# The first feed-forward layer in two batches, and attention prepared sequence by sequence

## The chip, the cores and the metric

The kernel runs on one core of a Trainium2 chip. TensorE (PE) multiplies matrices and transposes, VectorE (DVE), ScalarE (ACT) and GpSimd (POOL) work on tiles of 128 partitions, SyncE (SP) issues most transfers, and every engine takes its own instructions in order. Semaphores tie the engines together. The metric is the time of one execution on the device in microseconds, the median of several.

## The reference

The input x holds 8 sequences of 256 tokens with 128 features. Three layers follow one another, each on the layer-normalised x and added to x:

```
x = x + 0.5 * ffn(layernorm(x))
x = x + attention(layernorm(x))
x = x + 0.5 * ffn(layernorm(x))
```

`ffn` sends each token to one of 8 experts (the arg-max of a softmax over 8 gate logits), computes relu(x W1 + b1) W2 + b2 of that expert (hidden size 512) and scales it by the gate's probability. `attention` applies an RMS norm, makes q, k and v for 16 heads of 8 features, takes a causal softmax within each sequence, projects, and adds the normalised input.

## The kernel before

Tokens stand in 16 tiles of 128 (`row`, `x`, two tiles to a sequence).

**First feed-forward layer.** The 16 tiles are normalised, gated and routed in three chunks (`route_pick`, `route_prob`, `route_slot`). POOL writes each tile's rows to memory, sorted by expert (`dispatch`, L462), ScalarE pads every expert's region, and VectorE makes a table of at most 23 sorted tiles of one expert each (`tile_table`, NS = 16 + 8 - 1). TensorE fills the time until all have landed with products of zeros (`idle_work`, L1207: 35, then 9 after the landing).

**Expert tiles.** SyncE loads sorted tiles into a ring of 12 (L362). For tile t ScalarE normalises (L615), TensorE transposes (`turn`, L1271), ScalarE copies back (L621), TensorE multiplies by W1 in four pieces (`hidden`, L1279), ScalarE and VectorE apply the relu (L627, L923), TensorE multiplies by W2 (`output`, L1290), VectorE adds the bias (L939), scales and adds x (`scale`, L947, done one iteration later, after the bias of tile t + 1), and POOL scatters the tile's rows to `x_d` (L470). VectorE copies the weights three tiles ahead (L931). TensorE's order is turn(t + 2), hidden(t + 1), output(t). Transposed tiles go to banks 0 and 1, outputs to banks 6 and 7, in turns.

**Between.** When all rows are scattered, SyncE loads x back (L408). Five units of 2, 2, 4, 4, 4 tiles are normalised (statistics on VectorE L801, power on POOL L454), transposed (L1339), multiplied into q, k (`quad_qk`, L1346) and v (`quad_v`, L1354), split into three bf16 parts (L680, L687, L1014, L1028), stored to `sp_d` by SyncE (`split_stores`, L383 and L384, four issues a sequence) and loaded back as stacks (`stack_load`, L397, four issues a half).

**Attention.** Step b of 8 has two halves of six units. TensorE makes the transposed scores of sequence b (`scores_k`, L1408 and L1414) and, for the maxima, the scores of sequence b + 1 (`scores_q`, L1381 to L1393); VectorE takes maxima (L1038, L1042), POOL splits them (`max_split`), TensorE turns them (`turn_max`, L1445), ScalarE copies them and SyncE loads them as extra rows of the stack (`max_rows`, L402): the first scores_k of a half waits for that transfer. ScalarE takes exponentials (L723), POOL masks (L541), TensorE multiplies by v (L1432, L1436). Steps 1 to 4 are a hardware loop. POOL also adds up the residual (L500 to L504). SyncE's order in step b is: `max_rows(b, 1)`, `stack_load(b + 2, 0)`, `max_rows(b + 1, 0)`, stores of a later sequence where one is due, `stack_load(b + 2, 1)`.

**Second feed-forward layer.** Its routing runs beside the last steps, and 23 expert tiles follow.

## Time and profile before

| what | us |
|---|---|
| median of three runs | 322.5 (321.55 to 323.66) |
| span of the profiled execution | 319.3 |
| first expert tiles | 41.6 to 84.9 |
| attention steps 0 to 7 | 127.5 to about 240 |
| second expert tiles | 264.5 to 308 |
| busy in the span: TensorE, VectorE, POOL, ScalarE | 276.5, 214.5, 178.8, 159.7 |

The profile gives the times of every instruction in one execution; a row of a timeline is one instruction or a run of like ones, and a bracket at its end says how long its engine had been idle and what ended the wait. TensorE's rows end later than its next one begins, since products overlap; what a product costs TensorE is read from start to start. PEclk is the clock granted to TensorE, 1.00 for 2.4 GHz and 0.50 for 1.2 GHz.

### The profile page before, as it was taken

Reading aid. Unit: us, or ns where it says so; the run is one execution under the profiler, and the core shown is the slowest. Engines: PE = TensorE matmul, PEld = TensorE weight load, DVE = VectorE, ACT = ScalarE, POOL = GpSimd, SP = SyncE. Lnnn points to the kernel's source line nnn. Section 1 sums busy time; section 2 is a strip of 40 time slices with the busy share of each in tenths; the row PEclk is TensorE's granted clock in tenths of the full one; section 3 lists DMA queues with packets and bytes.
Section 4 is the critical chain, followed back from the end, with each engine's and each line's share of the span. In section 5 each row is a group of like instructions: output and inputs, shape, how many; then the busy total and the mean of one; then the engine's idle time right before and its main releaser. Section 6 shows DMA issues by size and latency. Waiting matters only on the chain.

```text
span 319.3 us, 7990 instructions
## 1 busy us (share of the span) xinstructions
PE 276.5 (87%) x2396; PEld 224.1 (70%) x2396; DVE 214.5 (67%) x691; ACT 159.7 (50%) x389; POOL 178.8 (56%) x319
## 2 busy tenths in 40 slices
PE   8573999999995776999999999998977699999960
PEld 8463999999994363656666566665646588999960
DVE  3877048788608759987666777776787555888850
ACT  2430076666204834586666667768541107666620
POOL 5577815554525201587777787788657730554551
PEclk9855999999999998799999999999976579999996
DMA  6973141220040731662524522110001143222100
GB/s 180 403 293 119 53 95 54 65 63 31 24 126 8 199 121 53 197 180 88 156 79 134 152 72 74 57 53 6 3 19 42 42 121 86 51 67 71 34 10 0
DMA packets 34387, 29.37 MB, mean 92 GB/s; under 512 B 4108, under 2 KB 28817, under 8 KB 34352
## 3 DMA queue, kind: packets, MB, share of 16 engines
q1 hardware_dynamic: 29696, 23.52, 24.6%
q0 software_dynamic: 2496, 4.27, 4.1%
q10 hardware_dynamic: 2160, 1.14, 1.4%
q8 instruction: 18, 0.29, 0.4%
q14 instruction: 17, 0.14, 0.2%
HBM read 17.08 MB, written 12.55 MB: 93 GB/s over the span
## 4 chain that ended last, share of the span: by engine, by line
PE 58%; POOL 11%; DVE 10%; issue 7%; DMA 5%; ACT 4%; POOLq 1%; ACTq 0%; SPq 0%; DVEq 0%
PE bank L1279 13%; PE bank L1290 12%; PE bank L1207 5%; PE bank L1436 3%; PE bank L1408 3%; PE bank L1384 3%; POOL pT L541 2%; POOL row L454 2%; PE bank L1381 2%; PE bank L1414 2%; PE bank L1271 2%; POOL disp_d L462 2%; PE bank L1240 2%; PE bank L1466 2%; PE bank L1389 1%
## 5 line engine op out<-in xcount | busy, mean ns | idle before, releaser
L723 ACT ACTIVATE pT<-bank 128x512 f32<-128x512 f32 x96 | 56.4, 599 | 36.2 <-PE bank L1414 25.2
L1207 PE MATMUL bank<-zero 128*128 128x128 f32 x298 | 43.2, 314 | 9.4 <-DVE rowi L916 4.7
L1279 PE MATMUL bank<-xsT,ew 128*128 128x128 f32 x368 | 48.8, 276 | 0.2
L1290 PE MATMUL bank<-experts,hT 128*128 x368 | 48.9, 276 | 0.0
L1207 PEld LDWEIGHTS bank<-zero 128*128 128x128 f32 x298 | 41.6, 227 | 10.1 <-DVE rowi L916 4.7
L1038 DVE TENSOR_REDUCE mh<-bank 128x2 f32<-128x512 f32 x64 | 42.1, 682 | 8.5 <-PE bank L1384 8.2
L541 POOL TENSOR_SCALAR_AFFINE_SELECT pT<-pT 128x512 f32<-128x512 f32 x62 | 39.8, 643 | 10.2 <-ACT pT L723 9.9
L1279 PEld LDWEIGHTS bank<-xsT,ew 128*128 128x128 f32 x368 | 44.7, 192 | 0.7 <-ACT xsT L621 0.3
L1290 PEld LDWEIGHTS bank<-experts,hT 128*128 128x128 f32 x368 | 44.8, 192 | 0.5 <-issue 0.3
L627 ACT ACTIVATE hT<-bank,ew 128x128 f32<-128x128 f32 x92 | 28.8, 364 | 28.9 <-PE bank L1279 28.9
L923 DVE TENSOR_SCALAR hT<-bank,ew 128x128 f32<-128x128 f32 x92 | 28.0, 346 | 20.2 <-PE bank L1279 18.9
L470 POOL DMA_INDIRECT out<-ys_sb,xs_sb x23 | 22.5, 980 | 30.8 <-DVE ys_sb L947 30.2
L462 POOL DMA_INDIRECT disp_d<-row,slot x32 | 31.6, 988 | 13.6 <-issue 9.4
L470 POOL DMA_INDIRECT x_d<-ys_sb,xs_sb x23 | 22.7, 986 | 25.8 <-DVE ys_sb L947 25.1
L615 ACT ACTIVATE xq<-xs_sb 128x128 f32<-128x128 f32 x46 | 22.6, 492 | 26.5 <-DMA xs_sb<-disp_d 26.5
L1042 DVE TENSOR_REDUCE mh<-bank 128x4 f32<-128x512 f32 x32 | 22.1, 690 | 18.8 <-PE bank L1393 18.6
L1408 PE MATMUL bank<-qz,ks 99*128 99x512 bf16 x64 | 25.2, 396 | 0.4 <-DMA qz<-mT 0.3
L1384 PE MATMUL bank<-ks,qz 96*128 96x256 bf16 x128 | 25.4, 281 | 0.0
L931 DVE TENSOR_SCALAR ew<-experts 128x644 f32 x46 | 22.2, 491 | 2.2 <-issue 1.6
L585 ACT ACTIVATE xn<-row 128x128 f32<-128x128 f32 x23 | 10.6, 490 | 24.2 <-DVE row L813 24.2
L1436 PE MATMUL bank<-pT,va 128*32 128x256 f32 x256 | 20.9, 398 | 1.8 <-DVE pT L1164 1.4
L939 DVE TENSOR_TENSOR yb<-bank,ew 128x128 f32<-128x128 f32 x46 | 13.4, 291 | 12.7 <-PE bank L1290 10.0
(133 smaller groups left out, 479.4 us busy)
## 6 DMA issues: line engine op xcount, KB each, us to landing
sp_d<-spl SPq DMA_DIRECT2D x32, 192.0 KB, 2.6
experts<-in_experts SPq DMA_DIRECT2D x8, 578.0 KB
qz<-sp_d SPq DMA_DIRECT2D x32, 96.0 KB
ks<-sp_d SPq DMA_DIRECT2D x32, 96.0 KB
xs_sb<-disp_d SPq DMA_DIRECT2D x46, 66.0 KB, 1.8
row<-in_x SPq DMA_DIRECT2D x4, 256.0 KB, 5.5
row<-x_d SPq DMA_DIRECT2D x4, 256.0 KB, 5.0
disp_d<-pad ACTq DMA_DIRECT2D x12, 66.0 KB, 2.3
```

What stands on the lines that cost most here:

```text
L462: pool.indirect_dma_start(disp_d[f][:, :], bass.IndirectOffsetOnAxis(ap=slot[:, t:t + 1], axis=0), row[:, t, :], None).then_inc(d_tok[f], 16)
L470: pool.indirect_dma_start(target[:, :], bass.IndirectOffsetOnAxis(ap=xs_sb[:, t % RING, ID:ID + 1].bitcast(U32), axis=0), ys_sb[:, t % OUT ...
L541: pool.affine_select(out=p_, in_=p_, pattern=[[0, 4], [1, P]], compare_op=ALU.is_ge, fill=0.0, base=0, channel_multiplier=-1).then_inc(a_p ...
L627: mm = act.activation(hT[:, par, c, :], bank[2 + 2 * par][:, c * P:(c + 1) * P], ACT.Relu, bias=ew[:, k, HID + c:HID + c + 1])
L723: act.activation(pT[:, u, :], bank[2 + u % 2][:, :], ACT.Exp, scale=SCALE).then_inc(a_e, 1)
L1038: dve.tensor_reduce(mh[:, half, 1, :, 2 * pp + w], bank[u % 2][:, :].rearrange("p (h n) -> p h n", h=2), AX.X, ALU.max).then_inc(a_mx, 1)
L1207: pe.matmul(bank[b][:, 0:P], zero[:, :], zero[:, :], start=True, stop=True)
L1279: mm = pe.matmul(bank[2 + 2 * (k % 2) + c // 2][:, (c % 2) * P:(c % 2 + 1) * P], ew[:, k % WRING, c * P:(c + 1) * P], xsT[:, k % 2, :], st ...
L1290: mm = pe.matmul(bank[6 + k % 2][:, 0:D], hT[:, k % 2, c, :], w2.rearrange("p a c -> p (a c)"), start=(c == 0), stop=(c == HC - 1))
L1384: mm = pe.matmul(ov[:, j, :], qz[k][0:SROWS, half, j, pair - 4 * half, P:T], ks[k][0:SROWS, pair, :], start=False, stop=True, **MM_BANK)
L1408: mm = pe.matmul(ov, ks[k][0:KROWS, pair, 0:P], qz[k][0:KROWS, half, :, pair - 4 * half, :], start=True, stop=True, **MM_BANK)
L1436: mm = pe.matmul(o[32 * h:32 * h + 32, pp * T:(pp + 1) * T], va[:, k, 0, 8 * j + pair, :], pT[:, 3 * pp + h // 2, j * T:(j + 1) * T], star ...
```

## The change

The 16 tiles of the first feed-forward layer go in two batches of 8, each with its own routing tables, pads and region in memory, and each with up to 15 expert tiles: 30 in one run instead of 23. Batch 1's dispatches, tables and pads are put among the first tiles of batch 0. The transposed tile has one bank (7) and the output one (6). Attention is prepared per sequence, not per unit: statistics on VectorE, power and the normalisation itself on POOL (`seq_normalise`), then transposes, q, k, v and the splits. Sequences 0 to 2 are prepared in tiles 19 to 28 of the run; their x is loaded back once the first 15 tiles are scattered. Sequences 3 to 7 are prepared within attention steps 0 to 4 (sequence b + 3 in step b), in banks 4 and 5, which attention uses too. The repeated copies of the splits in SBUF are dropped; a store of six parts and three of two replace four of three. The loop over steps is unrolled. In the diff, code for the routing tables, semaphore names and the late layer's renumbering is left out.

```diff
+BATCH = [(0, 8), (8, 16), (0, 16)]
+NS = [t1 - t0 + NE - 1 for t0, t1 in BATCH]
+G0 = [sum(NS[:f]) for f in range(len(BATCH) + 1)]
+HEAD = 3
+HEAD_AT = [20, 22, 24]
+HEAD_PE = [(21, 22, 23), (23, 24, 25), (25, 26, 27)]
...
# SyncE
+            def split_stores(b):
+                k = b % SPL
+                sp.wait_ge(q_s2, b + 1)
+                sp.wait_ge(q_spl, b + 1)
+                dst = sp_d[b * 2 * t_rows:(b + 1) * 2 * t_rows, :].rearrange("(m r) n -> r m n", r=P)
+                sp.dma_start(dst[:, 0:6, :], spl[:, k, :, :]).then_inc(q_std[b], 16)
+                for c, src in ((3, slice(0, 4, 3)), (4, slice(2, 6, 3)), (5, slice(0, 6, 5))):
+                    sp.dma_start(dst[:, 2 * c:2 * c + 2, :], spl[:, k, src, :]).then_inc(q_std[b], 16)
...
+            pad_rows(0, range(0, 4))
+            tile_loads(0, NS[0])
+            pad_rows(1, range(0, NE))
+            tile_loads(G0[1], G0[1] + RING)
+            all_scattered(NS[0])
+            reload(range(HEAD))
+            tile_loads(G0[1] + RING, G0[2])
             sp.wait_ge(static_s, 6)
-            split_stores(0, 1)
-            stack_load(0, 0, 0)
-            stack_load(0, 0, 1)
-            stack_load(1, 1, 0)
-            max_rows(0, 0, 0)
-            stack_load(1, 1, 1)
+            split_stores(0)
+            stack_load(0, 0)
+            stack_load(0, 1)
+            split_stores(1)
+            stack_load(1, 0)
+            stack_load(1, 1)
             split_stores(2)
-            stores = {(0, 0): (3,), (0, 1): (4,), (1, 1): (5,), (2, 1): (6,), (3, 1): (7,)}
+            all_scattered(G0[2])
+            reload(range(HEAD, B))
+            max_rows(0, 0)
             for b in range(B):
...
+                max_rows(b, 1)
+                if b + 2 < B:
+                    stack_load(b + 2, 0)
+                if b + 1 < B:
+                    max_rows(b + 1, 0)
+                if b + HEAD < B:
+                    split_stores(b + HEAD)
+                if b + 2 < B:
+                    stack_load(b + 2, 1)
...
# POOL
+            def seq_normalise(b):
+                ln_scale(1, b)
+                pool.wait_ge(ln_rs[1], b + 1)
+                for t in (2 * b, 2 * b + 1):
+                    i1 = pool.tensor_scalar(xn[:, t, :], x[:, t, :], mv[:, t, 0:1], rs[:, t:t + 1],
+                                            ALU.subtract, ALU.mult)
+                i1.then_inc(ln_xn[1], 1)
...
+            dispatch(0, 0, range(0, 4))
+            dispatch(0, 1, range(4, 8))
             stack_fill(1)
+            dispatch(1, 0, range(8, 11))
+            for g in range(G0[1]):
+                scatter_out(x_d, g)
+                if g < 5:
+                    dispatch(1, 0, range(11 + g, 12 + g))
+            for g in range(G0[1], G0[2]):
+                scatter_out(x_d, g)
...
+                if g in HEAD_AT:
+                    seq_normalise(HEAD_AT.index(g))
...
# POOL, attention step
-                if not isinstance(b, int):
-                    pool.tensor_tensor(turn[:, n:n + 1], zero[:, 0:1], zero[:, 0:1], ALU.add)
...
+                    if b + 4 < B and (half, n) == (1, 3):
+                        seq_normalise(b + 4)
             max_split(0, 0)
+            seq_normalise(HEAD)
...
# ScalarE, expert tiles (after tile g) and attention step
+            def head_work(g):
+                for b in range(HEAD):
+                    if g == HEAD_PE[b][1]:
+                        seq_split1(b)
+                    if g == HEAD_PE[b][1] + 1:
+                        seq_split2(b)
+                for b in range(HEAD):
+                    if g == HEAD_PE[b][0]:
+                        seq_copy(b)
...
+                    if b + HEAD < B:
+                        if (half, u) == (0, 5):
+                            seq_copy(b + HEAD)
+                        if (half, u) == (1, 1):
+                            seq_split1(b + HEAD)
+                        if (half, u) == (1, 4):
+                            seq_split2(b + HEAD)
...
# VectorE, expert tiles (after tile g) and attention
+            def early_work(g):
+                if g == 0:
+                    pad_table(1)
+                if 1 <= g <= 4:
+                    tile_table(1, g - 1)
+                for b in range(HEAD):
+                    if g == HEAD_AT[b] - 1:
+                        ln_stats(1, b)
+                    if g == HEAD_PE[b][1]:
+                        seq_rest(b)
+                    if g == HEAD_PE[b][2]:
+                        seq_vbias(b)
+                    if g == HEAD_PE[b][1] + 2:
+                        seq_split3(b)
...
+                    if b + HEAD < B:
+                        if (half, u) == (1, 2):
+                            seq_rest(b + HEAD)
+                        if (half, u) == (1, 5):
+                            seq_split3(b + HEAD)
+                    if 0 < b and b + HEAD - 1 < B and (half, u) == (0, 1):
+                        seq_vbias(b + HEAD - 1)
+                    if b + HEAD + 1 < B and (half, u) == (1, 3):
+                        ln_stats(1, b + HEAD + 1)
...
             for u in range(6):
                 max_unit(0, 1, u)
+                if u == 2:
+                    ln_stats(1, HEAD)
...
# TensorE
             gate_turn(0, 2)
+            logits(0, 2)
             gate_turn(0, 3)
-            logits(0, 2)
-            ranks(0, 1)
             logits(0, 3)
-            ranks(0, 2)
-            counts(0)
-            pe.wait_ge(r_row, 1)
-            idle_work(5, 35)
+            ranks(1, 0)
+            counts(1)
+            pe.wait_ge(r_sm[0], 2)
+            idle_work(6, 35)
             all_dispatched(0)
...
+            def seq_turn(b):
+                pe.wait_ge(ln_xn[1], b + 1)
+                need(pe, q_vc, b)
+                if b >= HEAD:
+                    need(pe, a_ot, 2 * (b - HEAD))
+                for t in range(2):
+                    mm = pe.transpose(bank[5 if b >= HEAD else 1][:, t * P:(t + 1) * P], xn[:, 2 * b + t, :], ident)
...
+            def head_work(g):
+                for b in range(HEAD):
+                    if g == HEAD_PE[b][1]:
+                        seq_qk(b)
+                    if g == HEAD_PE[b][2]:
+                        seq_v(b)
+                for b in range(HEAD):
+                    if g == HEAD_PE[b][0]:
+                        seq_turn(b)
+
+            expert_tiles(0, G0[2], head_work)
...
+                    if s_ < B and (half, u) == (1, 0):
+                        seq_qk(s_)
...
+                    if s_ < B:
+                        if (half, u) == (0, 4):
+                            seq_turn(s_)
+                        if (half, u) == (1, 5):
+                            seq_v(s_)
```

In `expert_tiles` the three `between` functions are called at the end of iteration g: on TensorE after output(g), on ScalarE after relu(g + 1), on VectorE after the weights of tile g + 3. `s_` is b + 3.

## Rows read from the trace of the kernel before

**Rows 1.** Busy time by stretch: stretch, us, PE, PEld, DVE, ACT, POOL, PEclk, DMA

```profile
41.60:85.00 43.40, 43.31 (x382) 42.90 (x383) 33.60 (x108) 27.88 (x89) 19.29 (x20) 1.00 0.21 56
...
173.40:186.80 13.40, 13.32 (x147) 8.47 (x143) 9.50 (x19) 8.78 (x18) 10.28 (x29) 1.00 0.41 120
```

**Rows 2.** Timelines of ACT, PE, DVE and POOL before the first tile

```profile
15.32 1.65 ACT L585 ACTIVATE xn<-row 128x128 f32<-128x128 f32 x4 [2.61 <-DVE row L813]
...
16.30 1.94 PE L1232 MATMUL bank<-cst,xn 128*128 128x128 f32 x8 [0.88 <-DVE xn L822]
...
19.84 1.85 PE L1240 MATMUL bank<-wg,gT 128*128 128x8 f32 x8
...
24.13 0.19 PE L1263 MATMUL bank<-cum,cb 128*128 128x8 bf16 x1 [0.21 <-DVE cum L869]
28.97 12.18 PE L1207 MATMUL bank<-zero 128*128 128x128 f32 x88 [4.65 <-DVE rowi L916]
...
21.73 0.23 DVE L845 TENSOR_TENSOR lg<-bank,b_gate 128x64 f32<-128x64 f32 x1 [0.84 <-PE bank L1240]
...
16.17 1.20 POOL L462 DMA_INDIRECT disp_d<-row,slot  x1 [2.46 <-DVE slot L889]
...
35.69 0.96 POOL L462 DMA_INDIRECT disp_d<-row,slot  x1 [0.30 <-issue]
```

**Rows 3.** The products of zeros (L1207) by stretch: PE, PEld, PEclk, DMA

```profile
32.00:33.00 1.00, 1.00 (x7) 1.00 (x7) 0.50 0.20 68
...
37.00:38.00 1.00, 1.00 (x12) 1.00 (x11) 1.00 0.20 68
```

**Rows 4.** Timelines of PE, DVE and POOL in a steady expert tile

```profile
63.63 0.27 PE L1271 MATMUL bank<-cst,xq 128*128 128x128 f32 x1
...
64.04 0.34 DVE L947 SCALAR_TENSOR_TENSOR ys_sb<-yb,xs_sb 128x128 f32<-128x128 f32 x1
...
65.15 0.98 POOL L470 DMA_INDIRECT x_d<-ys_sb,xs_sb  x1 [0.91 <-DVE ys_sb L947]
```

**Rows 5.** Chain, timelines and the page's mask group, last tile to step 0's end

```profile
83.98 0.91 PE bank L1290 x8
...
91.07 2.03 SPq L408 DMA_DIRECT2D row<-x_d  x4
...
95.53 0.48 DVE L801 BATCH_NORM_STATS2 st<-row 128x6 f32<-128x128 f32 x2 [8.81 <-DMA row<-x_d]
...
96.66 0.72 POOL L454 TENSOR_TENSOR row<-vs,mhalf 128x2 f32<-128x2 f32 x1
...
99.91 1.89 PE L1346 MATMUL bank<-xnT,wt 128*128 128x256 f32 x8
...
141.24 0.39 PE L1408 MATMUL bank<-qz,ks 99*128 99x512 bf16 x1
...
L541 POOL TENSOR_SCALAR_AFFINE_SELECT pT<-pT 128x512 f32<-128x512 f32 x62 | 39.8, 643 | 10.2 <-ACT pT L723 9.9
```

**Rows 6.** Timelines of PE, SP's queue and DVE around a step's start

```profile
181.59 0.38 PE L1408 MATMUL bank<-qz,ks 99*128 99x512 bf16 x1
...
188.36 0.38 PE L1408 MATMUL bank<-qz,ks 99*128 99x512 bf16 x1
...
179.56 0.37 SPq L383 DMA_DIRECT2D sp_d<-spl  x1
...
181.63 0.78 SPq L397 DMA_DIRECT2D qz<-sp_d  x1
...
185.23 0.78 SPq L402 DMA_DIRECT2D qz<-mT  x1
...
181.79 0.69 DVE L1042 TENSOR_REDUCE mh<-bank 128x4 f32<-128x512 f32 x1 [1.35 <-PE bank L1393]
```

**Rows 7.** Granted clock by stretch: PE busy, PEclk, DMA

```profile
111.00:114.00 3.00, 0.39 (x4) 1.00 0.48 113
...
126.00:127.00 1.00, 0.95 (x4) 0.50 0.35 98
```

## The prediction before the run

> **What bounds the kernel now.** I read the busy times by stage first, then each stage's timeline by engine, and the chain of waits last. In the first run of expert tiles TensorE is busy 43.31 of 43.40 us and VectorE 33.60 [rows 1]: 23 tiles from 41.6 to 84.89 [rows 5], 1.89 us each, and a tile costs what TensorE needs for it. An attention step is bound by TensorE too, 13.32 us busy of 13.40, with POOL and SyncE close behind it [rows 1]. Between the two lies a stretch where TensorE mostly waits: from the last tile product at 84.89 to the end of attention step 0 at 141.24, 56.35 us [rows 5]. There x comes back from memory and q, k, v are made, split, stored and reloaded. This stretch is what the change attacks. The reader should see that it fills the stretch with work put inside two stages that have no free TensorE time, and behind in-order queues.
>
> **The change, part by part.** All sums are against the profiled execution, whose span is 319.3 us; the runs' median, 322.5, is 3.2 above it.
>
> *Start of the first tile.* Before, 16 dispatches run until 36.65 [rows 2]; after, 8 are needed, and at 1.3 us each (the sixteenth starts at 35.69, the first at 16.17) the eighth is issued by 26.3 and has landed near 28. But TensorE's queue does not reach the tiles then. Batch 1's gates now stand before 35 idle products. From 15.3 the chain is: normalise four tiles on ScalarE 1.65, transpose four 0.97 (half of the eight), copy about 0.6, and the same again for the last four, then logits 1.85 [rows 2]; with two short waits this ends near 24.7. The pick then takes 2.4 us, from 21.73 to the counts at 24.13 in the old run [rows 2], so the idle products start near 27.3 (old: 28.97). They ran 7 records a us at half clock and 12 at full [rows 3], so 35 of them (70 records) take 8.2 us, some 4.4 of it at half clock as in the old run (30 records) and 3.5 at full; then 9 more, 1.55, and the first transposes, 0.63: first product at 37.7 against 41.6. **-3.9.** Bounds: -7.6 if the clock stays up for logits and idle products; -3 if the gates come late.
>
> *Seven more tiles.* 15 + 15 instead of 23, at 1.89: **+13.2.** The single banks 6 and 7 cost nothing: the bias of a tile is done 0.4 us after its product (63.63, and the scale behind it at 64.04 [rows 4]), and the next output product starts 1.0 after it; that cover goes if VectorE is more than 0.6 late. Batch 1's tables, about 3.2 us of VectorE in tiles 0 to 4, have 0.42 us of slack a tile (33.60 of 43.40 used [rows 1]): **+0.7**, 0 to 1.5.
>
> *Three sequences in tiles 20 to 29, TensorE's own work.* Two products for q and k 0.9 (1.89 for two sequences [rows 5]), v half as many columns, 0.45, two transposes 0.25 (1.94 for eight at half clock [rows 2]): 1.6 each, **+4.8**, nothing hides it. VectorE's and ScalarE's shares fit beside it.
>
> *The wait of TensorE for POOL.* Here is the first point of decision. `seq_normalise(0)` follows `scatter_out(20)` in POOL's program; that scatter waits for `scale(20)`, which VectorE does in iteration 21, after the bias of tile 21. TensorE asks for the result at once after output(21). In a steady tile TensorE goes on at 63.63, the scale of the tile before ends at 64.38, its scatter runs 65.15 to 66.13 [rows 4]: 2.5 us. Then POOL still has the shifted variance and power, about 1.0 (the power alone 0.72), and two 128x128 normalisations [rows 5]. These have no row. The nearest is the mask, one input, 128x512, at 0.64 [rows 5]: a quarter of it, 0.16, is the low end for each, all of it the high end; I take 0.4, between them, since the operation reads two scalars a row. So TensorE waits 2.5 + 1.0 + 0.8 + handovers = 4.4 us at tile 21. At 23 and 25 `seq_v` (0.45) is done first, but VectorE's wait for the split delays its scale by about as much: 4.3 each. **+13.0**, bounds 11.7 and 16. Behind the waiting transpose stand the whole next tile and, through it, ScalarE and VectorE; nothing covers it. The Trainium skill (SBUF — State Buffer, Who interferes with whom) says that a VectorE instruction that takes a second port and a GpSimd instruction block each other for the whole instruction. VectorE's weight copies stand beside these normalisations; an estimate by that page is one such copy more a wait, which speaks further against the change. No row here shows the pair, and the sum is made without it.
>
> So the tiles take 43.3 + 13.2 + 0.7 + 4.8 + 13.0 = 75.0, and the last product ends near T = 112.7, not 84.89.
>
> *From T to the end of step 0.* What is removed: the reload before any preparation (scatters landed at 91.07, x at 95.53 [rows 5]) and the five units' splits. Sequence 0's stack is loaded by T. But SyncE works through three stores (2.1 each) and four half stacks (3.0 each) [rows 6], with the landing between a store and its load, from `seq_split3(0)` on: it is free near T + 7.4. Then it reloads the last five sequences, about 2.0, and only then comes `max_rows(0, 0)`, at T + 9.4; scores_k start 3.1 later (185.23 to 188.36 [rows 6]), T + 12.5. VectorE meanwhile waits for x of sequence 3 between its maxima, until about T + 11 (reload 91.07 to 95.53). After the last maxima of sequence 0 step 0 starts at T + 12.9; its halves take 6.5 and, with the preparation of sequence 3, 6.6 + 1.35, so it ends at T + 27.4; I add 1.0 for half clock after the wait (at 126 the clock is 0.50 [rows 7]). That is 28.4 against 56.35: **-27.95**; bounds -30.5 and -25.
>
> *Five sequences inside steps 0 to 4.* TensorE's 0.9 + 0.45 stand in the second half, fully on its path: +1.35 a step (step 0's is counted above). The second point of decision is SyncE's order. Before, the stores of a later sequence are issued at 179.56, two us before the step ends at 181.59; the second half stack follows at 181.63, and the maxima's rows at 185.23; they land for the scores at 188.36 [rows 6], with no time to spare. After, `split_stores(b+3)` waits for `seq_split3`, behind VectorE's last maximum, which begins at 181.79 [rows 6] and ends 0.9 into the next step; `seq_v` puts that at 0.4. With the split's 0.6 and a handover the stores start at 1.15, take 2.07, the half stack 3.04: `max_rows` is issued at 6.26, not 3.64, and the second half of the step starts 3.1 later, at 9.3 instead of 6.77. **+2.55** in steps 1 to 5, in which the transposes (0.25) and POOL's later max split hide. Bounds: stores from 1.45 to 2.6 give 1.9 and 3.2. Steps 1 to 4: 4 x (1.35 + 2.55) = **+15.6**; step 5 **+2.55**. The loop's unrolling and the dropped `turn` operations are costed at nothing: TensorE leaves no free time in a looped step [rows 1], and the dropped operations stand before masks that wait for ScalarE; without that cover they are worth under 1 us a step. Steps 6 and 7 and the second feed-forward layer stay.
>
> Sum: -3.9 + 13.2 + 0.7 + 4.8 + 13.0 - 27.95 + 15.6 + 2.55 = +18.0. Span 337.3; with 3.2 for what lies around it, **340.5 us**.
>
> **The rivals.**
> *A, the forecast:* both waits bite. All lower ends together give about 329, all upper ends 352. 0.57.
> *B, the clock falls in each of the three waits:* each wait is 4.3 us without a product. For it: at 126 the clock was at half after some thin us. Against: over 111 to 114 TensorE was busy 0.39 of 3.00 and the clock stayed at 1.00 [rows 7]. It then takes about 4.4 us of products to come back, as from 28.97 on [rows 3], and loses half of them: 3 x 2.2 = 6.6, so 347. The Trainium skill (TensorE: Matmul & The Clock Gate, HAM oscillation — how this bites in real kernels) tells of kernels whose bursts of products alternate with waits and start each burst cold; by that page this is what should come. 0.15.
> *C, SyncE is not late:* the stores' issue is cheaper or the split earlier. Then POOL's order shows instead: `seq_normalise` (about 1.9 us) stands ahead of `max_split(b+1, 1)`, and the turn of the maxima, hardly waiting now, waits 1.1 more. Steps 1 to 4 cost 1.35 + 0.25 + 1.1 = 2.7 each, step 5 nothing: 340.5 - 7.4 = 333. 0.15.
> *E, TensorE does not wait in the tiles, SyncE is late:* 340.5 - 13.0 = 327.5. For it: only if POOL gets ahead of the scatters, which its order excludes as I read it. 0.05.
> *D, the other side, the preparation is hidden:* one mechanism, queues that keep up, so that x of a sequence is normalised before TensorE asks. It decides at the point where POOL ends 4.4 us earlier than computed; then the later half-step chains start early too. Tiles cost 18.7 more, steps 6.4, and the stretch after them still falls by 28: about 316. 0.08.
>
> **How the numbers follow.** The likeliest is A, 340.5. The range 327 to 351 takes in A's bounds but for its last us, B, C and most of E; outside are D, C's low end and a little above, under 0.2. About 1% is what a measurement of this kernel can tell from no change. Faster by over 1%: D without its upper part, 0.07. Within 1%: the rest of D, E's low part, C's low end, 0.08. Slower: 0.85.
>
> **What would show it.** In the profile after: the first product near 37.7; three idle times of TensorE of about 4.3 us in the tiles, released by POOL writing xn; last tile product near 113; step 0 ending near 141; in steps 1 to 5 a TensorE wait for the DMA of the maxima's rows near the middle, and step lengths of 17.2, then 15.9, then 13.3. Wrong would be: no POOL wait in the tiles (D, E), steps under 16 (C), or half clock in the tiles (B).

## The result, and the profile after

The changed kernel took **365.2 us** (median; 364.05 to 366.23) against 322.75 for the kernel before: ratio 1.131, 95% interval 1.126 to 1.136. It is 42.5 us slower. The direction was forecast, the size was not: 340.5 was 25 us too low, and the time lies above the range of 327 to 351. The profiled execution's span is 364.4 us (before 319.3; forecast 337.3), its mean granted clock 0.868 (before 0.916).

Where the 45.1 us between the two spans lie, against the forecast's own terms (us). The end of the last tile product is read as its start plus 0.91 for its eight records. In the kernel before that product starts at 84.85, so it ends at 85.76; 84.89, from which the prediction starts, is the end of the product ahead of it:

```profile
84.85 1.15 PE L1290 MATMUL bank<-experts,hT 128*128 x8
```

| stretch | before | forecast | after | after less forecast |
|---|---|---|---|---|
| start to first hidden product | 41.61 | 37.7 | 40.70 | +3.0 |
| first run of tiles | 44.15 | 75.0 | 87.7 | +12.7 |
| last product to the end of step 0 | 55.5 | 28.4 | 29.75 | +1.35 |
| steps 1 to 4 | 53.68 | 69.3 | 72.13 | +2.85 |
| step 5 | 13.23 | 15.8 | 18.25 | +2.45 |
| step 6 | 13.78 | 13.78 | 13.78 | 0 |
| step 7 to the end | 97.4 | 97.4 | 102.1 | +4.7 |

**The tiles.** The waits of TensorE between 80 and 150 us, grouped (what waited and for what: us in all, times, longest):

```profile
PE bank L1325 <- POOL xn L463: 15.0, 3, 5.2
PE bank L1378 <- DVE mh L1052: 4.5, 2, 3.8
PE bank L1439 <- POOL mb L540: 1.6, 1, 1.6
```

Three waits for POOL's normalised x, as forecast (13.0). The first of them in the timelines of TensorE and POOL (start, us, engine, line, in brackets the idle time before it); the scatter at 87.81 answers the one at 65.15 in [rows 4]:

```profile
91.62 0.69 PE L1325 MATMUL bank<-cst,xn 128*128 128x128 f32 x2 [5.20 <-POOL xn L463]
...
87.81 0.98 POOL L478 DMA_INDIRECT x_d<-ys_sb,xs_sb  x1 [0.80 <-DVE ys_sb L945]
88.87 0.19 POOL L453 TENSOR_SCALAR vs<-mv 128x2 f32<-128x2 f32 x1
89.14 0.72 POOL L455 TENSOR_TENSOR row<-vs,mhalf 128x2 f32<-128x2 f32 x1
89.97 1.59 POOL L463 TENSOR_SCALAR xn<-row,mv 128x128 f32<-128x128 f32 x2
```

The order is the one that the forecast read from POOL's program. Only the two normalisations take longer than forecast: 1.59 us, not 0.8. Behind the wait the clock is down, which answers [rows 7] with the other sign (stretch, us, busy time of PE, PEld, DVE, ACT, POOL, granted clock, DMA share, GB/s):

```profile
88.00:92.00 4.00, 0.38 (x2) 0.39 (x3) 0.12 (x2) 0.00 (x0) 3.29 (x5) 0.81 0.05 16
92.00:94.00 2.00, 2.00 (x11) 2.00 (x10) 0.00 (x0) 0.92 (x3) 0.00 (x0) 0.50 0.00 0
94.00:96.00 2.00, 2.00 (x11) 2.00 (x10) 0.64 (x3) 0.62 (x2) 0.00 (x0) 0.50 0.00 0
96.00:98.00 2.00, 2.00 (x10) 1.60 (x10) 0.92 (x3) 0.44 (x2) 0.70 (x1) 0.68 0.00 0
```

0.50 is the lower of the two levels, 1.2 of 2.4 GHz. Products run at it for 5.7, 6.1 and 3.0 us after the three waits, 14.8 in all, so about 7 us are lost. A smaller loss lies earlier, at tile 18: VectorE's copy of the weights takes 2.14 us instead of 0.49, beside POOL's fill of va (timelines of VectorE and POOL):

```profile
77.70 2.14 DVE L929 TENSOR_SCALAR ew<-experts 128x644 f32 x1
...
77.64 1.84 POOL L504 MEMSET va<- 128x2048 f32 x1
```

**The start.** Timelines of TensorE and ScalarE before the first tile, and two stretches of the products of zeros (columns as above):

```profile
27.06 12.62 PE L1196 MATMUL bank<-zero 128*128 128x128 f32 x88
40.54 0.33 PE L1261 MATMUL bank<-cst,xq 128*128 128x128 f32 x1 [0.75 <-ACT xq L625]
...
30.08 0.49 ACT L625 ACTIVATE xq<-xs_sb 128x128 f32<-128x128 f32 x1 [4.44 <-DMA xs_sb<-disp_d]
...
30.00:32.00 2.00, 2.00 (x11) 2.00 (x11) 1.48 (x4) 0.49 (x1) 1.32 (x1) 0.50 0.51 123
34.00:36.00 2.00, 2.00 (x20) 2.00 (x20) 0.00 (x0) 0.00 (x0) 0.47 (x1) 1.00 0.64 151
```

The first dispatched rows have landed and are normalised at 30.6, but TensorE works off idle products until 39.5.

**Before step 0.** SyncE's queue and TensorE's last wait before step 0, which starts at 143.12:

```profile
111.45 0.38 SPq L376 DMA_DIRECT2D sp_d<-spl  x1
115.59 0.94 SPq L389 DMA_DIRECT2D qz<-sp_d  x1
...
134.17 0.39 SPq L376 DMA_DIRECT2D sp_d<-spl  x1
...
137.18 2.43 SPq L366 DMA_DIRECT2D row<-x_d  x5
140.00 0.82 SPq L396 DMA_DIRECT2D qz<-mT  x1
...
142.29 0.61 PE L1378 MATMUL bank<-cb 128*128 128x512 bf16 x1 [3.78 <-DVE mh L1052]
```

From the first store (111.45) to the rows of the maxima (140.00) it is 28.5 us. SyncE issues transfers for most of it, with three gaps of 1.8 to 1.9 us, in which it waits for a store's landing (twice) and for the splits of sequence 1.

**In a step.** Step 2 starts at 175.88. POOL, TensorE and SyncE's queue in it, and step 5's wait (its rows of before are [rows 6]):

```profile
177.72 1.58 POOL L463 TENSOR_SCALAR xn<-row,mv 128x128 f32<-128x128 f32 x2
180.45 0.22 POOL L540 TENSOR_TENSOR mb<-mr,zero 128x16 bf16<-128x16 f32 x1
180.82 0.27 PE L1439 MATMUL bank<-cb,mb 128*24 128x128 bf16 x2 [2.12 <-POOL mb L540]
...
177.12 0.37 SPq L376 DMA_DIRECT2D sp_d<-spl  x1
182.55 0.78 SPq L396 DMA_DIRECT2D qz<-mT  x1
...
240.50 0.51 PE L1398 MATMUL bank<-qz,ks 99*128 99x512 bf16 x1 [2.76 <-DMA qz<-mT]
```

Both orders bite: POOL's max split comes 2.1 us late behind the normalisation, and SyncE issues the rows 6.67 us after the step's start (forecast 6.26, before 3.64). In steps 1 to 4 TensorE meets POOL first, and while it waits there most of SyncE's lateness passes; in step 5, which has no normalisation, it meets SyncE.

### The profile page after: what moved, and what is told of

It reads as the page before. It is cut to its first block, busy times and chain, and to the rows that moved or that the text cites. A ratio compares the mean times of both kernels' runs of the same rounds, so it can differ in the third digit from the quotient of the medians.

```text
span 364.4 us, 8006 instructions
## 1 busy us (share of the span) xinstructions
PE 296.2 (81%) x2420; PEld 239.5 (66%) x2420; DVE 224.8 (62%) x743; ACT 164.3 (45%) x417; POOL 197.3 (54%) x316
## 4 chain that ended last, share of the span: by engine, by line
PE 50%; POOL 14%; DVE 10%; issue 9%; SPq 6%; DMA 6%; ACT 2%; POOLq 0%; DVEq 0%; ACTq 0%
PE bank L1269 13%; PE bank L1283 12%; PE bank L1196 3%; POOL disp_d L472 3%; POOL pT L552 3%; PE bank L1430 3%; POOL row L455 2%; PE bank L1398 2%; POOL xn L463 2%; PE bank L1334 2%; SPq L378 2%; PE bank L1373 2%; DMA qz<-mT 2%; PE bank L1261 2%; SPq L389 2%
## 5 line engine op out<-in xcount | busy, mean ns | idle before, releaser
L1283 PE MATMUL bank<-experts,hT 128*128 x424 | 59.4, 285 | 1.5 <-DVE yb L937 1.2
L1269 PE MATMUL bank<-xsT,ew 128*128 128x128 f32 x424 | 59.2, 285 | 0.9 <-ACT xsT L631 0.9
L478 POOL DMA_INDIRECT x_d<-ys_sb,xs_sb x30 | 31.1, 1038 | 49.3 <-DVE ys_sb L945 45.3
L1269 PEld LDWEIGHTS bank<-xsT,ew 128*128 128x128 f32 x424 | 54.2, 200 | 2.5 <-ACT xsT L631 1.1
L1283 PEld LDWEIGHTS bank<-experts,hT 128*128 128x128 f32 x424 | 53.6, 198 | 3.4 <-issue 2.5
L1052 DVE TENSOR_REDUCE mh<-bank 128x2 f32<-128x512 f32 x64 | 42.5, 682 | 19.2 <-PE bank L1373 18.9
L637 ACT ACTIVATE hT<-bank,ew 128x128 f32<-128x128 f32 x106 | 33.2, 364 | 32.9 <-PE bank L1269 32.9
L1196 PE MATMUL bank<-zero 128*128 128x128 f32 x190 | 31.8, 344 | 1.2 <-POOL zero L435 1.1
L929 DVE TENSOR_SCALAR ew<-experts 128x644 f32 x53 | 27.5, 526 | 8.1 <-issue 7.8
L1196 PEld LDWEIGHTS bank<-zero 128*128 128x128 f32 x190 | 30.6, 256 | 1.4 <-POOL zero L435 1.1
L937 DVE TENSOR_TENSOR yb<-bank,ew 128x128 f32<-128x128 f32 x53 | 15.2, 287 | 14.1 <-PE bank L1283 13.1
L631 ACT COPY xsT<-bank 128x128 f32<-128x128 f32 x53 | 14.0, 264 | 13.4 <-PE bank L1261 13.2
```

The source lines that it names most:

```text
L478: pool.indirect_dma_start(target[:, :], bass.IndirectOffsetOnAxis(ap=xs_sb[:, g % RING, ID:ID + 1].bitcast(U32), axis=0), ys_sb[:, g % OUT ...
L637: mm = act.activation(hT[:, g % 2, c, :], bank[2 + 2 * (g % 2)][:, c * P:(c + 1) * P], ACT.Relu, bias=ew[:, g % WRING, HID + c:HID + c + 1])
L1052: dve.tensor_reduce(mh[:, half, 1, :, 2 * pp + w], bank[u % 2][:, :].rearrange("p (h n) -> p h n", h=2), AX.X, ALU.max).then_inc(a_mx, 1)
L1196: pe.matmul(bank[b][:, 0:P], zero[:, :], zero[:, :], start=True, stop=True)
L1269: mm = pe.matmul(bank[2 + 2 * (g % 2) + c // 2][:, (c % 2) * P:(c % 2 + 1) * P], ew[:, g % WRING, c * P:(c + 1) * P], xsT[:, g % 2, :], st ...
L1283: mm = pe.matmul(bank[6][:, 0:D], hT[:, g % 2, c, :], w2.rearrange("p a c -> p (a c)"), start=(c == 0), stop=(c == HC - 1))
```

## The experiments

All start from the changed kernel; the diffs are against it. Ratios are to the kernel before, so the changed kernel's 1.131 is the mark.

### The waits in the tiles, and what stands behind them

**e1_no_wait.**

```
-HEAD_PE = [(21, 22, 23), (23, 24, 25), (25, 26, 27)]
+HEAD_PE = [(23, 24, 25), (25, 26, 27), (27, 28, 29)]
             for g in range(G0[1], G0[2]):
+                if g in HEAD_AT:
+                    seq_normalise(HEAD_AT.index(g))
                 scatter_out(x_d, g)
...
-                if g in HEAD_AT:
-                    seq_normalise(HEAD_AT.index(g))
...
```

> POOL normalises a sequence before it scatters the tile, and TensorE asks for it two tiles later. Both theories expect the three waits of TensorE for POOL in the tiles (15.0 us together) and the half clock behind them (about 6.5 us) to be gone, so the last product of the tiles falls from 128.4 to about 107. Theory P (the time is set by TensorE in the tiles and then a fixed stretch to step 0): the whole kernel gets 21 us faster, ratio to the changed kernel's 365 about 0.94. Theory S (behind the tiles SyncE's chain of three stores and four half stacks sets the start of step 0, 28.5 us from the first store at 111.45 to the rows of the maxima at 140.0): the first store moves only from 111.45 to about 103, and step 0 starts with it, so 8 to 9 us are gained and the idle stretch before step 0 grows by 12.

358.0 us, ratio 1.111 (1.102 to 1.120). The last product of the tiles came at 106.8 instead of 128.4, with the clock at 1.00 throughout: the stretch of tiles is 20.9 us shorter. Step 0 started only 10.6 us earlier, at 132.47. TensorE's wait before it, and SyncE's first store and its rows:

```profile
131.64 0.61 PE L1378 MATMUL bank<-cb 128*128 128x512 bf16 x1 [8.91 <-DVE mh L1052]
...
100.60 0.38 SPq L376 DMA_DIRECT2D sp_d<-spl  x1
...
129.58 0.82 SPq L396 DMA_DIRECT2D qz<-mT  x1
```

The first store moved to 100.60, and from there to the rows it is 29.0 us again. Half of what the tiles gave went into a longer wait behind them (VectorE here waits for x of sequence 3, which SyncE reloads just ahead of the rows). That is theory S. The tiles gave 5.9 us more than the 15.0 of the waits, which fits the about 7 us of half clock behind them.

**e8_prelude** changes that order alone.

```
-            reload(range(HEAD))
+            reload(range(HEAD + 1))
...
             stack_load(1, 0)
+            max_rows(0, 0)
             stack_load(1, 1)
             split_stores(2)
             all_scattered(G0[2])
-            reload(range(HEAD, B))
-            max_rows(0, 0)
+            reload(range(HEAD + 1, B))
```

> Before step 0 the rows of the first maxima are sent after the third half stack, ahead of the fourth, of the stores of sequence 2 and of the reload; x of sequence 3 comes back with the first three sequences. Theory S (SyncE's chain sets step 0): the rows are issued right after the maxima's copy at 135.7, not at 140.0, VectorE does not wait for x of sequence 3 (3.3 us), and step 0 starts 4 to 5 us earlier; with less half clock 4 to 7 us are gained. If something else is late (stack of sequence 1, products of step 0): under 2 us.

362.3 us, ratio 1.120 (1.115 to 1.126). The rows went out at 135.67, step 0 started at 139.15, 4.0 us earlier; 2.9 us of it show in the time, where its interval just meets the changed kernel's.

**e9_chain** is both.

> The edits of e1_no_wait and e8_prelude together: no wait in the tiles, and the rows of the first maxima ahead of the fourth half stack, the stores of sequence 2 and the reload. Alone they moved the start of step 0 from 143.1 to 132.5 and 139.2, that is by 10.6 and 4.0. Theory S (behind the tiles SyncE's chain sets step 0): together they give more than the sum, since e1 left a VectorE wait of 8.9 us for x of sequence 3; the rows can go out behind the third half stack, near 121, and step 0 starts at 123 to 125, 18 to 20 us earlier than in the changed kernel; the whole gains 16 to 20 us. If the two only add up, step 0 starts near 128.5 and 12 us are gained.

348.7 us, ratio 1.080 (1.076 to 1.085): 16.5 us gained, where the two alone gave 7.2 and 2.9. Step 0 started at 124.54, 18.6 earlier against 10.6 + 4.0. SyncE's rows:

```profile
120.96 0.79 SPq L396 DMA_DIRECT2D qz<-mT  x1
```

Each edit alone uncovers the other's delay. The chain of stores, half stacks, reload and rows on SyncE is the bound between tiles and attention as soon as the tiles stop waiting.

**e2_fill_wait** keeps TensorE busy during the waits.

```
                     if g == HEAD_PE[b][0]:
+                        need(pe, q_r, b)
+                        idle_work(0, 28)
                         seq_turn(b)
```

> Adds 28 idle products (nothing reads them) in front of each of the three transposes that wait for POOL; the waits stay as long. If the loss behind the waits is the clock alone: the tiles after each wait run at full clock again, the last tile product comes about 6.5 us earlier (122 instead of 128.4), and the kernel gains 5 to 6.5 us. If the tiles behind the waits are slow for another reason (late weights, late transfers): no gain, within 1 us.

In the trace the clock stays up (columns as above):

```profile
92.00:94.00 2.00, 2.00 (x20) 2.00 (x20) 0.41 (x2) 1.32 (x5) 0.00 (x0) 1.00 0.03 8
```

From the first hidden product to the last product it took 83.8 us instead of 87.7: 3.9 us for the clock, at least, since the idle products overshoot the wait (TensorE no longer waits for xn). Step 0 started 3.85 earlier, the span is 5.0 shorter. In the times, 363.0 us and ratio 1.129 (1.123 to 1.135), this can't be told from the changed kernel. So the clock's part rests on the trace.

**e3_va_early** moves two fills.

```
             pool.wait_ge(ids_s, 1)
             dispatch(0, 0, range(0, 4))
...
-                if g == G0[1]:
-                    pool.memset(va[:, :, :, :, :], 0.0).then_inc(static_s, 1)
-                    pool.wait_ge(static_s, 5)
-                    pool.memset(va[:, :, :, :, HD:HD + 1], 1.0).then_inc(static_s, 1)
```

(The three lines stand ahead of the `ids_s` wait instead.)

> The two fills of va stand before the dispatches instead of between the scatters of tiles 15 and 16. If VectorE's weight copy of 2.14 us (0.49 otherwise) is held by POOL's fill of 1.84 us beside it: that copy takes 0.5 us, TensorE's wait of 0.9 us behind it goes, and the kernel gains 1 to 2 us. If the copy was slow for another reason (the reload's transfers at the same time): it stays above 1 us and nothing is gained.

The copy of tile 18 takes 0.49 us (VectorE's timeline below). The output product behind it starts 1.97 us after the one before, not 3.36: 1.4 us less. The whole stretch of tiles is 1.9 us shorter (85.8).

```profile
78.03 0.49 DVE L928 TENSOR_SCALAR ew<-experts 128x644 f32 x1
```

364.1 us, ratio 1.129 (1.121 to 1.137): the gain is in the trace, and in the times too small to tell.

### The start

**e4_few_idle.**

```
             pe.wait_ge(r_sm[0], 2)
-            idle_work(6, 35)
+            idle_work(6, 4)
             all_dispatched(0)
             idle_work(6, 9)
```

> 35 idle products before the dispatches' landing become 4. If the idle products, not the landing, set the first tile now: the first hidden product moves from 40.70 to about 32 and the kernel gains 7 to 8.5 us. If the clock needs them: the first tiles run at half clock, 1.0 to 1.7 us longer each for some three tiles, and the gain is 4 to 5 us. If the landing sets it: no gain.

358.3 us, ratio 1.116 (1.108 to 1.123): 7.0 us gained. The first hidden product on TensorE's timeline:

```profile
34.22 1.06 PE L1269 MATMUL bank<-xsT,ew 128*128 128x128 f32 x8
```

It is 6.5 us earlier than in the changed kernel, and the clock is at 1.00 from 34 us on (in the changed kernel from 33). The idle products had covered a landing that the change itself brought forward.

### The steps

**e5_sp_order** and **e6_act_norm** change one queue each, **e7_both** both.

```
e5:
                 max_rows(b, 1)
+                if 0 < b and b + 2 < B:
+                    split_stores(b + 2)
...
-                if b + HEAD < B:
-                    split_stores(b + HEAD)
e6 (POOL, then VectorE, then ScalarE):
-                    if b + 4 < B and (half, n) == (1, 3):
-                        seq_normalise(b + 4)
+                    if b + 4 < B and (half, n) == (1, 0):
+                        ln_scale(1, b + 4)
...
+                    if b + HEAD + 1 < B and (half, u) == (0, 4):
+                        ln_stats(1, b + HEAD + 1)
                     if b + HEAD + 1 < B and (half, u) == (1, 3):
-                        ln_stats(1, b + HEAD + 1)
+                        ln_bias(1, b + HEAD + 1)
...
+                    if b + HEAD + 1 < B and (half, u) == (1, 5):
+                        act.activation(xn[:, t, :], x[:, t, :], ACT.Identity, bias=nb[:, t:t + 1], ...
```

> SyncE stores the splits of sequence b+3 after the rows of the maxima of the next step's second half, not before; nothing else changes. The sum of the prediction (2.55 us in each of steps 1 to 5 is SyncE's lateness): 12 us gained. The theory after the trace (two queues late together: in steps 1 to 4 POOL's max split, behind the normalisation, is asked for first and stays): the wait for the rows in step 5 (2.8 us) and those of 0.7 us in steps 1 and 4 go, steps 1 to 4 stay above 17.5 us, 3 to 5 us gained.

> The normalisation of sequences 4 to 7 (1.58 us a step) moves from POOL to ScalarE, with its statistics half a step earlier; POOL keeps only the power (1.0 us), in a place with time to spare. If POOL alone was the bound in steps 1 to 4: the four waits of 2.1 us and the half clock behind two of them go, 9 to 12 us gained. If SyncE stands right behind it (rows of the maxima issued 6.67 us after the step's start and landing about 3 later, the second half starting at 9.8 instead of 10.1 to 10.5): 1 to 3 us gained, and the wait shows up at the second half's first scores, for the DMA.

> Both edits together. If the two queues hide each other: more than the sum of the two alone; steps 1 to 5 fall from 17.7 to 18.4 us to about 15 (13.33 as before, 1.35 for the two products and v, 0.25 for the transposes), 13 to 15.5 us gained. If there is a third limit (ScalarE or VectorE in the step): steps stay above 16, 8 to 10 us gained.

| | us | ratio (interval) | steps 1 to 5, us |
|---|---|---|---|
| changed kernel | 365.2 | 1.131 (1.126 to 1.136) | 17.7, 18.4, 18.4, 17.7, 18.3 |
| e5, SyncE's order | 359.0 | 1.111 (1.106 to 1.117) | 17.1, 18.2, 15.2, 19.7, 15.3 |
| e6, ScalarE normalises | 367.1 | 1.135 (1.129 to 1.141) | 20.9, 20.3, 20.6, 20.5, 16.4 (of an execution of 372.4 us) |
| e7, both | 349.4 | 1.083 (1.076 to 1.090) | 15.6, 15.8, 15.2, 15.3, 14.5 |

TensorE's waits in the steps of the three (156 to 240 us), grouped; first e5:

```profile
PE bank L1439 <- POOL mb L540: 6.4, 4, 2.1
PE bank L1398 <- DMA qz<-mT: 1.5, 1, 1.5
```

then e6, with the queue's row and the wait in its step 2 (start 177.43). The execution that was profiled took 372.4 us, 5.3 more than the median, so the place of the wait is read from it, and not what the edit costs:

```profile
PE bank L1406 <- DMA qz<-mT: 12.1, 4, 3.4
...
184.12 0.78 SPq L396 DMA_DIRECT2D qz<-mT  x1
...
186.99 0.61 PE L1406 MATMUL bank<-qz,ks 99*128 99x512 bf16 x1 [2.63 <-DMA qz<-mT]
```

then e7:

```profile
PE bank L1406 <- DMA qz<-mT: 3.7, 5, 1.2
```

One edit gained 6.2 us, the other nothing (367.1 against 365.2, within the intervals), both together gained 15.9. With POOL out of the way the rows are issued 6.7 us after the step's start, exactly as late as with it: two queues had been late side by side, and TensorE's wait for the first covered the one for the second. That e6 should gain nothing was in neither theory. In its profiled execution TensorE's wait for SyncE's rows was 2.6 to 3.4 us in steps 1 to 4, and each second half behind it took 10.6 to 10.8 us (7.8 in the changed kernel), with TensorE busy throughout at a mean granted clock of 0.71 to 0.72. In the changed kernel, behind waits of 2.1 us for POOL, the first halves of steps 2 and 3 stand at 0.84 and those of 1 and 4 at 1.00. Whether the clock falls as often in e6's other executions, no trace shows.

**Which order on SyncE?** Three more kernels. e10_steps puts the rows ahead of both half stacks; e14_steps2 sends them on ScalarE's queue and leaves SyncE the changed kernel's order; e16_steps3 sends the rows of the first halves on ScalarE's queue, and on SyncE the stores ahead of both half stacks.

```
e10, SyncE's loop:
     max_rows(b, 1)
+    split_stores(b + 2)
+    max_rows(b + 1, 0)
     stack_load(b + 2, 0)
-    max_rows(b + 1, 0)
-    split_stores(b + HEAD)
     stack_load(b + 2, 1)
e14, SyncE's loop, and in ScalarE's max_copy:
-    max_rows(b, 1)
     stack_load(b + 2, 0)
-    max_rows(b + 1, 0)
     split_stores(b + HEAD)
     stack_load(b + 2, 1)
...
+    act.wait_ge(a_mtc, 2 * b + half + 1)
+    act.dma_start(qz[b % 2][MROW:MROW + 3, half, :, :, :]..., mT[:, half, :]).then_inc(a_m[half], 16)
e16, SyncE's loop (steps to 5); ScalarE sends the rows of (b + 1, 0) as in e14, after its copies:
     max_rows(b, 1)
+    split_stores(b + 2)
     stack_load(b + 2, 0)
-    max_rows(b + 1, 0)
-    split_stores(b + HEAD)
     stack_load(b + 2, 1)
```

All three have e6's normalisation on ScalarE.

> As e7_both, but the rows of the maxima of the next step's first half go ahead of the half stack that waits for the stores' landing. e7 left steps 1 to 5 at 15.6, 15.8, 15.2, 15.3, 14.5, with a TensorE wait of 0.8 to 1.2 us for those rows at each step's start (3.7 us in all). If that is SyncE's order too: the waits go and the steps come to 14.7 to 15.0, 3 to 4 us less than e7. If the half stacks then come late instead: second halves longer than 8.0, nothing gained against e7.

> The rows of the maxima go out on ScalarE's DMA queue, right behind the copy that they wait for, and the normalisation of sequences 4 to 7 is ScalarE's too; SyncE keeps stores and half stacks in the changed kernel's order. If SyncE's queue alone was left of the lateness in e7_both (steps of 15.6, 15.8, 15.2, 15.3, 14.5): steps 1 to 5 come to 14.8 to 15.0 (TensorE's own work in them is 14.8), 17 to 18 us gained against the changed kernel. If ScalarE now is late (two issues and two waits for its own copy a step, some 1.6 us more on it): steps of 15.5 to 16.5, 10 to 14 us gained.

> In the steps alone: normalisation of sequences 4 to 7 on ScalarE (as e7_both); SyncE sends the rows of a step's second half, then the stores, then both half stacks, so that no half stack stands behind the stores that is wanted in the next half; the rows of the next step's first half go out on ScalarE's queue after its copies, where 4 us are left. If the steps are a matter of queue orders alone: first halves 6.8, second halves 7.9 to 8.2, steps 14.7 to 15.1 (TensorE's own work is 14.8), 17 us gained against the changed kernel, 1 to 2 more than e7_both. If a landing or ScalarE is the limit: second halves above 8.5, no better than e7_both.

379.6 us (1.172; 1.163 to 1.180), 371.2 (1.152; 1.146 to 1.158) and 349.9 (1.082; 1.075 to 1.089). TensorE's waits in the steps, e10, then e14, then e16:

```profile
PE bank L1377 <- DMA ks<-sp_d: 18.5, 5, 4.1
```

```profile
PE bank L1371 <- DMA ks<-sp_d: 11.7, 5, 2.5
```

```profile
PE bank L1414 <- DMA qz<-mT: 1.8, 4, 1.1
```

In e10 the first half stack comes late (first halves 11.8 to 13.7 us), in e14 the second, behind the stores (second halves 9.3 to 12.6). Both missed what was expected by 15 us and more. In e16 neither half stack comes late: steps of 15.0, 15.1, 15.2, 14.7, 15.0. The first three of them, all engines (columns as above):

```profile
158.35:173.32 14.97, 14.78 (x154) 9.87 (x152) 11.85 (x29) 11.28 (x25) 10.69 (x24) 1.00 0.36 109
173.32:188.41 15.09, 14.79 (x153) 9.95 (x153) 11.93 (x30) 11.21 (x24) 10.44 (x24) 1.00 0.35 107
188.41:203.58 15.17, 14.95 (x152) 9.88 (x153) 11.72 (x29) 11.05 (x24) 10.28 (x24) 1.00 0.35 106
```

TensorE is busy 14.8 of 15: 13.3 as before and 1.5 for the sequence's own products and transposes (forecast 1.35 and 0.25). So the steps' excess over that was queue order, with the half clock behind its waits. e16's time is no better than e7's: its steps 1 to 5 are 1.5 us shorter together, its step 0 is 1.1 longer.

### The second feed-forward stage

From step 7 to the end the changed kernel takes 102.1 us, the kernel before 97.4. **e11_late** sets four small orders back, **e13_late2** also the wait on each register load, **e17_align** does something else alone:

```
e11:  SyncE reads the first tile rows ahead of its wait for the landing; norm(g0 + 1) ahead of copy_T(g0);
      TensorE reads the experts behind output(g); bank[6 + g % 2] and bank[0] in the last run
e13:  e11, and
+                            if g == G0[tables_of(g)]:
                                 dve.wait_ge(r_te, tables_of(g) + 1)
e17:
-  nt, ns, gs = ..., slice(G0[f], G0[f + 1])
+  nt, ns, gs = ..., slice(G0[f] + f, G0[f + 1] + f)
-  loaded(..., te[0:1, l0:l1], NE - 1)
+  loaded(..., te[0:1, l0 + tables_of(g):l1 + tables_of(g)], NE - 1)
...   (and SyncE's loads from rowi in the same way)
```

> Four small orders are set back to those of the kernel before, all else stays: SyncE reads the first tile rows ahead of its wait for the landing, ScalarE normalises the second tile ahead of the first copy, TensorE reads the experts' numbers behind the last product and not ahead of the next, and the last 23 tiles have two output banks. If these make the second feed-forward layer's stage slower than before (from step 7's start to the end 102.1 us, against 97.4): it falls to 97.5 to 98.5 and the kernel gains 4 to 5 us, of it up to 1 us in the first tiles. If it is the clock or the transfers: under 1.5 us.

> As e11_late, and the register loads of the experts' numbers (on VectorE and TensorE, for every four tiles) wait for the table's semaphore only for the first tile of a run, as in the kernel before; in the changed kernel each carries that wait, long met. In the trace VectorE stands 0.69 us before the copy behind such a load, 0.15 in the kernel before. If the wait on the load costs that: tiles come to 1.89 to 1.90 us each, without one of 2.0 to 2.5 in four; step 7's start to the end falls from 102.1 to 98.5 or below, and the kernel gains 4 to 6 us. If it is the code's length or the clock: tiles of 2.0 to 2.5 stay, under 1.5 us gained.

> Only the columns of the two tables are moved: those of the second run of tiles start at column 16, not 15, those of the last at 32, not 30, so that each register load of four numbers starts at a multiple of 16 bytes, as all did in the kernel before. If a load that starts elsewhere is slower: VectorE's 0.69 us before the copy behind a load fall to about 0.15 in the later runs, tiles come to 1.89 to 1.90 each, the last 23 tiles and the second run of 15 are 1 to 2 us shorter together, 1 to 2.5 us gained. If not: no change, within 0.7 us, and the tiles of 2.0 to 2.2 stay.

e11 took 366.3 us (1.138; 1.132 to 1.142), e13 366.0 (1.136; 1.129 to 1.143): nothing gained, against 4 to 6 expected. From the last dispatch to the last run's first product it took 7.2 us in both, 8.25 in the changed kernel and 6.1 in the kernel before, so the orders at the start give 1 us. It is lost again behind: from the first output product of the last run to the last it took 44.0 us in both, against 43.1 and 41.2. The tiles of other lengths among those of 1.89 stayed: 2.0 to 2.2 us in the changed kernel, and up to 2.5 in these two. e17 took 362.3 us (1.116; 1.107 to 1.126). Behind its last run's first tile its tiles come every 1.89 to 1.90 us but for the last two, and the 43.1 us become 42.2. VectorE's register loads in the last run (309 to 351 us; count, then shortest, median and longest in ns), and its idle time ahead of the copies that follow them, the changed kernel, then e17:

```profile
L308 DVEq TENSOR_LOAD <-te x5: 745/1101/1135, 312.9 to 344.9; - x5
DVE ew L929 <- issue: 3.7, 5, 0.9
```

```profile
L308 DVEq TENSOR_LOAD <-te x5: 340/344/750, 312.1 to 342.4; - x5
DVE ew L929 <- issue: 0.5, 1, 0.5
```

The tables' columns start at 0, 15 and 30 in the changed kernel and at 0, 16 and 32 in e17, so there a load of four numbers starts at a multiple of 16 bytes of its table. The fifth load in this window has three numbers; it takes 0.75 us in either kernel. From step 7 to the end e17 needs 100.1 us, 2.0 less than the changed kernel. At most 1.4 of it can be the edit's: 0.94 from the first output product to the last, and 0.4 from the last dispatch to the first load, where SyncE reads the second table. The rest comes earlier, in routing that the edit doesn't touch; e7 and e16, which leave the whole stage as it is, need 100.9 and 100.6. The last kernel below, which has e13's and e17's edits, needs 98.2.

### All together

**e12_all**, **e15_all2** and **e18_all3** put the edits together, each with what was known by then.

> All edits together: few idle products, fills of va early, normalisation ahead of the scatter with TensorE asking one tile later, SyncE's order before step 0 and in the steps, normalisation on ScalarE in the steps, the late orders. By theory S with the measured terms: first product 34, last product of the first run of tiles near 96, step 0 starting near 111 (first store near 90, then stores, half stacks and rows as in e9_chain), steps 14.5, 4 x 14.9, 14.5, two of 13.7, then 97.7 to the end: a span near 310 to 314, 2 to 3% faster than the kernel before. If SyncE cannot start its chain earlier than e9_chain did: step 0 near 118 and a span near 320, no faster than before.

> All together: few idle products, fills of va early, normalisation ahead of the scatter with TensorE asking a tile later, x of sequence 3 early, the stores of sequences 1 and 2 between the half stacks, rows and normalisation of the steps on ScalarE, the late orders with loads that wait once. By theory S: step 0 starts at 112 to 114 (117.4 in e12_all), steps of 14.8 to 15.0, two of 13.8, 98 us from step 7 to the end: a span of 311 to 316, 1 to 2.5% faster than the kernel before. If the packed preparation costs more than it gives even so: a span above 320.

> All mended: 8 idle products at the start instead of 44, fills of va early, normalisation ahead of the scatter and asked for a tile later, x of sequence 3 early, the second half stack of sequence 0 on ScalarE's queue, the stores of sequences 1 and 2 early on SyncE's, idle products that hold the clock before step 0, the steps as in e16_steps3, tables as in e17_align, the late orders. By the terms: step 0 starts near 112 (114.5 in e15_all2), steps 14.5, 4 x 15.0, 14.6, 13.6, then 97.5 to 99 to the end: a span of 312 to 315, 1.5 to 2% faster than the kernel before. If there is a further cost in the change that the terms miss: a span above 320, no faster.

357.4 us (1.093; 1.087 to 1.098), 345.8 (1.074; 1.068 to 1.080), and **315.6 us, ratio 0.976 (0.971 to 0.981)**, for e12, e15 and e18. e12 had e10's order in the steps, e15 that of e14; with steps of 18 to 21 us both missed their sum. e18 has e16's order in the steps and e17's tables. Before step 0 SyncE has this order, and ScalarE's queue takes the second half stack of sequence 0 and the first rows of the maxima:

```
             split_stores(0)
             stack_load(0, 0)
-            stack_load(0, 1)
             split_stores(1)
+            split_stores(2)
             stack_load(1, 0)
             stack_load(1, 1)
-            split_stores(2)
             all_scattered(G0[2])
-            reload(range(HEAD, B))
-            max_rows(0, 0)
+            reload(range(HEAD + 1, B))
```

It is 2.4% faster than the kernel before. Its stretches (first product to last of the tiles, to step 0, steps 0 to 5, the rest; columns as above):

```profile
32.49:97.38 64.89, 63.97 (x541) 62.05 (x541) 53.93 (x185) 41.51 (x129) 43.57 (x48) 1.00 0.31 85
97.38:111.83 14.45, 11.16 (x96) 8.99 (x94) 9.36 (x20) 0.36 (x1) 4.87 (x11) 1.00 0.62 185
111.83:201.88 90.05, 85.38 (x874) 55.84 (x873) 69.27 (x159) 63.92 (x132) 62.95 (x141) 1.00 0.34 104
201.88:313.60 111.72, 91.85 (x778) 79.34 (x778) 72.33 (x264) 50.71 (x139) 58.25 (x80) 0.85 0.15 43
```

TensorE is busy 63.97 of 64.89 us in the tiles at full clock, and step 0 starts at 111.83, 15.7 us before that of the kernel before. Side by side with the kernel before (us; here the tiles are read to the end of their last record):

| stretch | before | e18 | difference |
|---|---|---|---|
| start to first hidden product | 41.6 | 32.5 | -9.1 |
| first run of tiles | 44.4 | 64.9 | +20.5 |
| to step 0 | 41.5 | 14.45 | -27.1 |
| steps 0 to 5 | 80.6 | 90.05 | +9.4 |
| step 6 to the end | 111.1 | 111.8 | +0.65 |

So with the orders mended the change as a whole pays, in three parts. The start gives 9.1: 8 dispatches instead of 16 stand before the first tile, and 8 idle products are left. The moved preparation gives 27.1 behind the tiles and costs 9.4 in the steps and 7.3 in the tiles. The seven more tiles of the two batches cost 13.2, more than the moved preparation leaves; without the start there would be no gain. No run has one of these parts without the others. In the changed kernel the orders cost more than all of it gives.

## Why the prediction was wrong in size

**What held.** That TensorE waits three times for POOL, where, and behind what; that SyncE's stores push the rows of the maxima back, to 6.67 us (forecast 6.26); that the stretch behind the tiles falls by 28 (25.7 measured); that a step's own work grows by 1.6 (1.5); that the change is slower. Rivals D (all hidden) and E (no wait) are out.

**What failed.** In the main, one step: the loss of clock behind a wait was kept apart as rival B and priced at nothing in the forecast's sum for the tiles, where it costs about 7 us. The other steps are two late queues in the attention steps that were taken as alternatives, a stage set down as "stay", a size taken from another operation, and a rate and an end misread from rows. Each follows, with what it measured.

**Start, -3.9: measured -0.9.** The step that failed is the rate of the idle products. "7 records a us at half clock and 12 at full" came from one-us stretches [rows 3], in which a record that reaches over an edge counts in full. From start to start a record took 0.213 us at half clock and 0.111 at full, 4.7 and 9.0 a us. The row of the same 88 records in the kernel before, 12.18 us, stands in [rows 2]; the forecast made 9.75 of it, and 12.6 came. Another 0.5 is a wait of the second transpose for ScalarE's second tile. That the products, not the landing, now set the start was read rightly; e4 shows that they could go, for 7 us.

**Waits for POOL, 13.0: measured 15.0.** The term mis-sized is the normalisation: 0.8 us each, not 0.4. The mask's 0.64 for four times the columns was taken as the upper end, and the truth lies above it. The copies of weights that the prediction saw beside these normalisations are not there in the changed kernel: VectorE stands still with TensorE. In e1 a copy overlaps the first pair of them: it takes 0.58 us instead of 0.49, and the second of the pair 1.01 instead of 0.79.

**Rival B was not a rival.** It was given 0.15 as another way than A, but it comes on top of A: 5 us without a product each time, then 0.50. Its price, 6.6, fits what the runs show: 14.8 us of products at half clock, 5.9 us gained beyond the waits in e1, and 3.9 at the least in e2. The Trainium skill (TensorE: Matmul & The Clock Gate, HAM oscillation — how this bites in real kernels) says that bursts between waits start cold; the trace agrees, at 0.50 after each of the three waits. The forecast had set one stretch of the kernel before against it, where the clock had stayed up [rows 7].

**Tables and early tiles, +0.7: measured +2.4.** From the first hidden product to the end of tile 21's output product it took 45.5 us, 43.1 in the kernel before. Tile 18 with the fill of va is 1.4 of it (e3). About 0.5 goes when the register loads are moved to other columns (e17), and about 0.5 lies in tiles 3 to 7, beside the tables.

**The misread end, 0.9.** The forecast read the end of the tiles before at 84.89, one output product early (85.76). So it counted 0.9 us too few in the tiles and as much too many in the stretch behind them; the time that it forecast for that stretch, 28.4, doesn't rest on it.

**Last product to step 0's end, 28.4: measured 29.75.** Right in size and in what it named. What the forecast did not say: this term belongs to SyncE, not to the tiles. It was tied to T, the end of the tiles, but it runs from the first store. As the tiles were late, both fitted; in e1 they came apart by 10 us.

**Steps 1 to 5: 2.55 each was not the whole.** A and rival C (POOL's max split late) were again treated as alternatives. They stand side by side: TensorE waits for POOL first, and that wait covers most of the one for SyncE's rows. Taking POOL's lateness away alone gains nothing (e6), SyncE's alone 6.2 us (e5), both 15.9 (e7). In steps 2, 3 and 5 half clock comes on top: 18.4 and 18.3 us.

**Second feed-forward layer, "stay": +4.7.** Costed at nothing because its work is the same. But its helper functions were rewritten for the batches. Of the 4.7, 2.0 lie in the output products of the 23 tiles (43.1 us against 41.2) and 2.15 between the last dispatch and the first product (8.25 against 6.1). Where a table starts is 0.9 of the first (e17), the orders at the start 1 of the second (e11). With both in e18 all but 0.8 of the 4.7 is gone, though e11's orders alone lost in the tiles what they gave at the start. Beside e17's columns that loss is gone; why stays open.

So of the 27 us of span that the sum missed, 12.7 lie in the tiles (clock 7, the normalisation 2.0, the fill and the early tiles 1.7 more than forecast, the misread end 0.9, one wait for the single output bank 0.6), 5.3 in the steps, 4.7 in the last stage, 3.0 in the start, 1.35 before step 0.

## What to carry to other kernels

When work is moved into a stage whose engine waits, write down for each in-order queue when it can start that work and what stands behind it, and take every queue that is late, not the first: two late queues hide each other, in the forecast and in the experiments, where one fix alone gains 6 us, the other nothing, and both 16 us. Treat the loss of clock behind a wait as part of the wait's price, not as another case. And read a stage that "stays" in the diff: rewritten helpers change orders, and where a table starts, even when the work is the same.

## What the runs showed of the hardware that was not expected

- A POOL fill holds up a VectorE copy that starts beside it: 2.14 us beside a fill of 1.84, 0.49 when the fill is moved (e3). The Trainium skill (SBUF — State Buffer, Who interferes with whom) says that a VectorE instruction in a mode that takes a second port and a GpSimd instruction lock each other out for the whole instruction. The trace agrees, for a POOL instruction that only writes; which ports this copy takes, no row shows.
- POOL takes 0.79 us for a 128x128 subtract and multiply with two numbers a row, more than for its 128x512 mask (0.64).
- VectorE's register load of four numbers takes 0.34 us where it starts at a multiple of 16 bytes of its table (e17, last run) and 1.0 to 1.1 where it doesn't (changed kernel, last run), and VectorE stands idle for 0.7 to 0.9 us behind the second kind. A load of three numbers takes 0.75 us in either kernel. Alignment is what e17 changes; why it matters, no run shows.
- Taking one of two late queues away gained nothing (e6): the wait moved to the other queue, and in the execution that was profiled the granted clock was 0.71 to 0.72 over the half step behind each such wait.
